# Expert layers of a two-layer Perceiver block: first products, their sums with bias and activations kept four deep, the second product one job later, and function tables called for at the heads of stages

## The reference, cut to what matters

```
def _L0_ffn_ref(x, Wg, alpha, ln_w, ln_b, fc1_w, fc1_b, fc2_w, fc2_b):
    top_vals, top_idx = jax.lax.top_k(logits, TOP_K)
    ...
    for e in range(Wg.shape[1]):
        hdn = _layernorm(xf, ln_w[e], ln_b[e])
        a = jax.nn.gelu(hdn @ fc1_w[e] + fc1_b[e], approximate=True)
        y = a @ fc2_w[e] + fc2_b[e]
        out = out + y * comb[:, e:e + 1]
```

## Time and profile before

| | us |
|---|---|
| median of 3 runs | 1574.12 |
| lowest and highest run | 1567.26, 1579.7 |
| profiled execution, its own time | 1572.63 |
| its span, first to last instruction | 1570.8 |
| busy PE, PE weight loads, DVE, ACT, POOL | 1264.7, 1097.8, 996.1, 841.9, 835.7 |
| mean granted clock of PE | 0.899 of full speed |

### The profile page before, as it was taken

The page is one execution under the profiler, slowest core; times in us unless marked ns, Lnnn a source line. Parts: engine busy times, 40 slices in busy tenths (PEclk is TensorE's granted clock), DMA queues, the critical chain, the costliest instruction groups (busy, mean ns, idle before and its releaser), DMA issues. The chain is left out here.

```text
span 1570.8 us, 48801 instructions
## 1 busy us (share of the span) xinstructions
PE 1264.7 (81%) x15330; PEld 1097.8 (70%) x15331; DVE 996.1 (63%) x3247; ACT 841.9 (54%) x2658; POOL 835.7 (53%) x1700
## 2 busy tenths in 40 slices
PE   3877788989729996799999999999969878449991
PEld 2655777878629886577777777777758767349991
DVE  4655367877346664577777777777759888433334
ACT  1555256565314443577777777777737665224450
POOL 2555024666636564466666666666534566646661
PEclk9999578788559998899999999999979999569996
DMA  7998552121112121312111111111000000122215
GB/s 223 261 263 218 213 165 76 58 63 53 35 49 73 59 62 37 113 62 91 33 50 33 50 34 43 40 37 43 15 15 3 16 24 23 45 61 68 70 58 169
DMA packets 91997, 122.01 MB, mean 78 GB/s; under 512 B 12689, under 2 KB 67218, under 8 KB 91858
## 3 DMA queue, kind: packets, MB, share of 16 engines
q1 hardware_dynamic: 74194, 82.77, 17.8%
q0 software_dynamic: 12288, 34.82, 7.4%
q10 hardware_dynamic: 5376, 2.63, 0.6%
HBM read 89.68 MB, written 30.49 MB: 76 GB/s over the span
## 5 line engine op out<-in xcount | busy, mean ns | idle before, releaser
L1592 ACT ACTIVATE p_prob<-six,p_nm 128x257 f32<-128x257 f32 x512 | 236.4, 475 | 132.1 <-DVE p_nm L1634 122.2
L1634 DVE TENSOR_REDUCE p_nm<-six 128x2 f32<-128x514 f32 x256 | 164.8, 686 | 12.9 <-PE six L1495 12.8
L1842 PE MATMUL bank<-sb_w,m_experts_aT 128*128 x1152 | 156.6, 279 | 7.6 <-ACT m_experts_aT L1871 4.9
L1821 POOL DMA_INDIRECT expert_outputs<-m_experts_y,m_experts_dest x144 | 142.7, 991 | 25.9 <-POOL m_experts_tiny L1820 11.4
L1858 PE MATMUL six<-m_experts_xT,m_experts_w 128*128 128x128 f32 x1152 | 156.0, 279 | 0.0
L1516 PEld LDWEIGHTS six<-sb_const,p_prob 128*128 128x128 f32 x1024 | 109.5, 141 | 65.5 <-issue 59.1
L1516 PE MATMUL six<-sb_const,p_prob 128*128 128x128 f32 x1024 | 137.0, 277 | 19.3 <-issue 17.5
L1842 PEld LDWEIGHTS bank<-sb_w,m_experts_aT 128*128 128x128 f32 x1152 | 141.1, 193 | 13.0 <-issue 12.8
L776 POOL DMA_INDIRECT expert_inputs<-p_r_x,p_r_slot x128 | 126.0, 984 | 41.2 <-issue 34.5
L1375 POOL TENSOR_TENSOR p_score<-p_score,p_mx 128x512 f32<-128x512 f32 x64 | 67.2, 1049 | 147.8 <-DVE p_mx L1320 145.9
L1858 PEld LDWEIGHTS six<-m_experts_xT,m_experts_w 128*128 128x128 f32 x1152 | 143.3, 196 | 0.6 <-issue 0.2
(11 more groups left out here) (287 smaller groups left out, 3498.2 us busy)
## 6 DMA issues: line engine op xcount, KB each, us to landing
ctxN_ring<-ctxN POOLq DMA_DIRECT2D x32, 516.0 KB, 10.6
ctxT_ring<-ctxT SPq DMA_DIRECT2D x32, 514.0 KB, 12.4
p_ctxT<-ctxT SPq DMA_DIRECT2D x32, 514.0 KB, 3.6
m_experts_x<-expert_inputs SPq DMA_DIRECT2D x144, 64.5 KB
bd_scores<-p_rows SPq DMA_DIRECT2D x32, 256.0 KB, 2.8
p_bd<-bd_scores SPq DMA_DIRECT2D x32, 256.0 KB
sb_w<-w SPq DMA_DIRECT2D x32, 256.0 KB
p_y<-expert_outputs SPq DMA_DIRECT2D x32, 128.0 KB, 3.3
```

What stands on the lines that cost most here:

```text
L1592: last = nc.scalar.activation(prob[:, b, g, :], scores_ps[:, g, 0:CTX], ACT.Exp, bias=nm[:, b % 2, g:g + 1], accum_out=total[:, b % 2, g:g ...
L1634: nc.vector.tensor_reduce(nm[:, b % 2, g:g + 2], scores_ps[:, g:g + 2, 0:CTX], AX.X, ALU.max, negate=True).then_inc(s[most], 1)
L1821: nc.gpsimd.indirect_dma_start(m.ys_dram[:, :], bass.IndirectOffsetOnAxis(ap=dest[:, t.par:t.par + 1], axis=0), y[:, t.par, :], None).then ...
L1842: last = nc.tensor.matmul(ps[6 + t.two][:, 0:D], aT[:, t.two, f * P:(f + 1) * P], m.w2[:, DS(held[p] + f * D, D)], start=(f == 0), stop=(f ...
```

## The change

`SECOND` goes from 4 to 5, so S and y of a job come one slot later; POOL's scatter follows (`at(SECOND + 2)`). `h` and `aT` get four buffers instead of two, and F writes banks 2 to 5 in turn instead of 2 and 3; the waits that guard them look four jobs back (`DEEP`). `w` and `xT`, and the banks of T and S, stay two deep. DVE reads 12 values for a group of eight jobs instead of 11, PE 8 as before.

In each `experts` stage and in `cross_many_heads`, ACT gets one more instruction at the head of its queue, a gelu or an Exp of one column of constants into `first_use`, which nothing reads.

```
+            nc.scalar.activation(first_use[:, :], c[:, 0:1], ACT.Exp)
...
-    FIRST, SECOND, STAGES = 1, 4, 6
+    FIRST, SECOND, STAGES, DEEP = 1, 5, 7, 4
...
-        tiny = sb("tiny", [P, 1])
-        w, h, aT = (sb(n, [P, 2, F]) for n in ("w", "h", "aT"))
+        tiny, first_use = sb("tiny", [P, 1]), sb("first_use", [P, 1])
+        w, h, aT = sb("w", [P, 2, F]), sb("h", [P, DEEP, F]), sb("aT", [P, DEEP, F])
+        deep = lambda t: t.par % DEEP
...
-                t = at(6)
+                t = at(SECOND + 2)
...
-                        last = nc.tensor.matmul(ps[6 + t.two][:, 0:D], aT[:, t.two, f * P:(f + 1) * P],
+                        last = nc.tensor.matmul(ps[6 + t.two][:, 0:D], aT[:, deep(t), f * P:(f + 1) * P],
...
-                    if t.past(2):
-                        pe.wait_ge(s["h" if biased else "aT"], t.before(2))
+                    if t.past(DEEP):
+                        pe.wait_ge(s["h" if biased else "aT"], t.before(DEEP))
                     for f in range(FC):
-                        last = nc.tensor.matmul(ps[2 + t.two][:, f * P:(f + 1) * P], w[:, t.two, f * P:(f + 1) * P],
+                        last = nc.tensor.matmul(ps[2 + deep(t)][:, f * P:(f + 1) * P], w[:, t.two, f * P:(f + 1) * P],
...
+            nc.scalar.activation(first_use[:, :], m.const[:, 0:1], gelu)
...
-                    if t.past(2):
-                        act.wait_ge(s["y_ps"], t.before(2))
-                    nc.scalar.activation(aT[:, t.two, :], h[:, t.two, :] if biased else ps[2 + t.two][:, :],
+                    if t.past(DEEP):
+                        act.wait_ge(s["y_ps"], t.before(DEEP))
+                    nc.scalar.activation(aT[:, deep(t), :], h[:, deep(t), :] if biased else ps[2 + deep(t)][:, :],
...
-                    if t.past(2):
-                        dve.wait_ge(s["aT"], t.before(2))
+                    if t.past(DEEP):
+                        dve.wait_ge(s["aT"], t.before(DEEP))
```

More of the change, by code:

```diff
@@ L1442, in cross_many_heads @@
         nm, total = (sb(n, [P, 2, G]) for n in ("nm", "total"))
+        first_use = sb("first_use", [P, 1])
         recip = sb("recip", [P, 2, G])
@@ L1912, in work @@
                     dve.wait_ge(s["h_ps"], t.nth())
-                    if t.past(2):
-                        dve.wait_ge(s["aT"], t.before(2))
+                    if t.past(DEEP):
+                        dve.wait_ge(s["aT"], t.before(DEEP))
                     by_chunk = lambda ap: ap.rearrange("p (f n) -> p f n", f=FC)
-                    nc.vector.tensor_tensor(by_chunk(h[:, t.two, :]), by_chunk(ps[2 + t.two][:, :]),
+                    nc.vector.tensor_tensor(by_chunk(h[:, deep(t), :]), by_chunk(ps[2 + deep(t)][:, :]),
                                             m.bias[:, DS(held[p + SECOND - 2] + D, FC)].unsqueeze(2).broadcast_to(
```

## The result

| | before | after |
|---|---|---|
| median of 6 runs each, us | 1573.45 | 1589.9 |
| lowest and highest | 1567.26, 1579.7 | 1585.79, 1595.79 |
| profiled execution, its span | 1572.63, 1570.8 | 1591.97, 1590.2 |

The ratio is 1.0107, with a 95% interval of 1.0082 to 1.0132. The change makes the kernel slower by 16 to 17 us. I had forecast 1564.7 us and a range up to 1573, and had given slower by over 1% a chance of 0.05.

The account below looks back on a forecast made before the run. PE's weight loads set the pace, but layer 0's experts lag 12.36 us because second products wait for gelu behind DVE's pauses. Gain 8.9 less 1.0 for stage ends is 7.9: 1572.6 to 1564.7 us, range 1558 to 1573.

Parts of the forecast that it names:

- What is late next: Layer 0 experts: once gelu's wait goes, DVE's w delays the first product; 3.5 us of the 12.36 stay.
- the prediction's own sign: Prediction wrong if the first product waits for w in most slots, or layer 0's jobs 3 to 71 stay over 140 us.
- Layer 1: I take 0: Layer 1 experts: no gain, bounds 0 and 0.5 us; a doubled head of PE would cost about 4 us over both layers.
- the pauses of DVE reach nobody in layer 1: Layer 1 experts: there is no h and ACT reads PSUM itself, so DVE's pauses hold up no engine.
- 8.9: Layer 0 experts: PE ends the stage 8.9 us sooner, 12.4 at most and 5.4 at least.
- the prediction's own sums: Layer 0 group heads: w costs 0.1 us now, 0.13 more with 12 values; 0.24 for each of 8 heads, 1.9 us.
- The table loads: Expert stages and cross attention: all three loads of 1.28 us are hidden already, so moving them gives 0.
- the estimate of 8.0 us: Three table switches at the skill page's 2.66 us each, load and drain; not taken, since the trace shows no drain.
- the end of the stages: Both expert stages: three second products in a row delay the last scatter by 0.6 and 0.4 us; cost 1.0, bounds 0 and 1.5.
- C: Rival for layer 0: w takes over and heads and pauses pass to PE in full, 17.8 us for 11.4; 1580.0 us; chance 0.06.
- A: Rival: everything goes, pauses never reach w and table loads were on the path; gain 12.4 plus 3.8, 1556.4 us; chance 0.14.
- B: Rival: nothing to be seen, layer 0's gaps have another cause or later stages give the gain back; 1572 to 1574 us; chance 0.15.

Follow-up runs that it names:

- a1_aligned: Changed kernel with every table entry moved one place (AROUND 9), so reads start at 8 half + 4 again; 1572.74 us, ratio 0.9959.
- d1_pe_read: Changed kernel with PE alone reading 12 values from the aligned place 8 half, DVE still 12 from 8 half + 3; ratio 1.0147.
- e1_control: The kernel before, unchanged, run and profiled once more; 1575.43 us, ratio 1.0014.
- e4_changed_again: The changed kernel, unchanged, run once more beside the kernel before on the same chip; 1591.24 us, ratio 1.0121.
- b3_heads: The kernel before with only the three calls for function tables at the heads of stages added; 1575.73 us, ratio 0.9995.
- e3_order_alone: The kernel before with only the second product one job later and reads held aligned (AROUND 9), two buffers, no table calls; 1567.57 us, ratio 0.9957.
- c1_late_two: a1_aligned with two buffers instead of four, the second product still one job later; 1526.0 us on another chip, ratio 0.9969.
- d2_dve_read: Changed kernel with DVE alone reading 16 values from the aligned place 8 half, PE still 8 from 8 half + 3; ratio 1.0095.
- e2_place_two: The kernel before with AROUND 6, so each group's reads start at 8 half + 2; 1595.46 us, ratio 1.0145.
- b1_shifted: The kernel before with its table one place further (AROUND 9), so reads start at 8 half + 5; 1598.95 us, ratio 1.0128.

## Why the prediction was wrong

**The step that failed** is in the part What is late next: "DVE will read 12 values instead of 11: by 1.47 / 11, 0.13 us more". I took a read's price as proportional to its number of values, and took PE's read, "8 as before" in the account of the change, as free of change. In fact the change moved where both reads start, and that I had before me: `experts_of` has `SECOND` in it twice, in the window's length, which I counted, and in its start, which I didn't. Measured, DVE's read went from 1.336 to 2.851 us and PE's from 0.593 to 1.986. For DVE's eight heads the term was 8 times 0.13, 1 us; for PE there was none. The two reads together cost 12.3 us of layer 0's steady part (a1_aligned). By the prediction's own sign it is wrong: the distance in layer 0 stayed over 140 us.

The second wrong number follows from it: "Layer 1: I take 0", with a gain as the only bound and a doubled head as an aside. Layer 1 lost 8.6 us. A PE at 99% has no cover for anything at its queue's head, so its steps there needed as careful a reading as DVE's. That the pauses of DVE reach nobody in layer 1 is wrong too: DVE's slow read alone costs 7.0 us there (d1_pe_read), through w.

**The ledger** of the two profiled spans, 19.4 us:

| part | after less before, us |
|---|---|
| layer 0, first transpose to last second product's end (154.62, 157.69) | +3.1 |
| layer 1, the same (142.25, 149.99) | +7.7 |
| last scatter behind it, layers 0 and 1 | +1.75, +1.4 |
| start of the cross attention stage | +1.2 |
| gap ahead of the second experts (44.7, 45.8) | +1.1 |
| second self attention (188.7, 192.6) | +3.9 |

These come to about 20.1 us; small differences in other stages take off the rest. The last two rows lie within what the control shows without any change (45.6 and 194.4 us), and the second self attention's is chance by the pair e1_control and e4_changed_again. In the first row two things of opposite sign stand together: the slow reads cost 12.3 us of layer 0's steady part (146.83 less a1_aligned's 134.50), and the rest of the change gains 7.8 there (142.33 less 134.50), both across chips.

**Right, point by point.** That second product, gelu and h stop layer 0, and that one job more of distance takes that away: the waits put down to gelu fall from 4.5 us (8 times) to 1.0 (3 times) in a1_aligned, and with the reads aligned the stage comes to 134.5 us, as forecast. The weight loads of the second product show it better. Their waits in layer 0's steady part, before and in a1_aligned:

```profile
PEld bank L1842 <- issue: 10.3, 21, 1.3
PEld bank L1846 <- issue: 3.0, 6, 0.6
```

Term by term: from the first transpose to the end of the last second product a1_aligned needs 145.01 us, 9.6 less than before, where I had 8.9; 7.8 of them lie in the steady part. But the credit is not all mine: DVE's read, aligned and of 12 values, takes 0.86 us against the 1.34 of 11 before, which gave back 0.48 us at each head that I had not counted. By the prediction's own sums w was late by 0.1 to 0.24 us at each of 8 heads, so 1 to 2 us of the gain is an estimate of what that gave. The kernel before with an aligned read of 12 values was not run, so no run separates it from the order. Layer 1 stays at 130.85 in a1_aligned. The table loads give nothing (b3_heads); the estimate of 8.0 us that I had worked out from the Trainium skill, ScalarE: Activation LUTs, section What ACT_TABLE_LOAD costs, would have been a ratio of 0.995, below the interval's low end of 0.9963. The calls stand where I said, the load at the head of the stage and first work unmoved by it. ACT's timeline in layer 0:

```profile
458.95 1.28 ACT L1869 ACT_TABLE_LOAD   x1 [18.95 <-PEq L1995]
460.25 0.20 ACT L1869 ACTIVATE m_experts_first_use<-sb_const 128x1 f32<-128x1 f32 x1
462.09 0.28 ACT L1884 ACTIVATE m_experts_xT<-six 128x128 f32<-128x128 f32 x1 [1.64 <-PE six L1854]
```

**Mis-sized: the end of the stages.** I had 0.6 and 0.4 us for the last scatter's falling behind. It started 0.85 and 1.11 us after the end of the last second product before, and 2.60 and 2.52 in the changed kernel: 1.75 and 1.41 us. POOL's timeline at the end of layer 1:

```profile
1553.31 0.98 POOL L1825 DMA_INDIRECT expert_outputs<-m_experts_y,m_experts_dest  x1 [0.16 <-issue]
1555.14 0.18 POOL L1824 TENSOR_TENSOR m_experts_tiny<-sb_const 128x1 f32<-128x1 f32 x1 [0.85 <-DVE m_experts_y L1908]
1555.48 0.98 POOL L1825 DMA_INDIRECT expert_outputs<-m_experts_y,m_experts_dest  x1 [0.16 <-POOL m_experts_tiny L1824]
1556.49 0.20 POOL L1824 TENSOR_TENSOR m_experts_tiny<-sb_const 128x1 f32<-128x1 f32 x1
1556.85 0.98 POOL L1825 DMA_INDIRECT expert_outputs<-m_experts_y,m_experts_dest  x1 [0.16 <-issue]
```

The scatters do come 1.37 us apart at the closest, but POOL idled for 0.85 us ahead of the last but one, for y. So DVE was late as well; why, no run shows. In a1_aligned's layer 0, where no read stands in the way, DVE idles for 1.96 us there, with two y made back to back:

```profile
606.83 0.29 DVE L1905 TENSOR_TENSOR m_experts_y<-bank,sb_bias 128x128 f32<-128x128 f32 x1 [0.23 <-PE bank L1846]
609.07 0.49 DVE L1905 TENSOR_TENSOR m_experts_y<-bank,sb_bias 128x128 f32<-128x128 f32 x2 [1.96 <-PE bank L1846]
```

**The rivals.** C gave 1580 us and the right sign. It isn't what happened: its mechanism was DVE's usual pauses passing to w, and with those pauses in place and the reads aligned the stage is quicker, not slower. What it had right is that w is next in line for DVE's lateness, which d1_pe_read shows. A and B fell with the forecast.

**Left open.** Why a1_aligned's layer 0 stays 3.7 us behind its layer 1, and e3_order_alone's 3.1, where c1_late_two on its chip shows 0.5. How much of the gain is the order's and how much the quicker read of 12 values. What makes DVE pause by 1 to 2 us away from the heads. The start of the cross attention stage, where POOL's first use of loaded data comes 2.0 to 4.2 us after the load's start in different kernels, with no relation to the edit that I can see (2.55 before, 2.03 in e3_order_alone, 3.75 in the changed kernel). And whether the limit is a table place divisible by four or an address divisible by 16 bytes: the table's own place in memory was not varied, only the place within it, and of the places that aren't divisible by four only 8 half + 2, 3 and 5 were tried.

## What to carry to other kernels

When a pipeline's depth changes, look for every address that is worked out from it, register reads at loop heads above all. Hold their start at a multiple of four values by padding the table; rather read a few values too many than start off the multiple. And if PE or DVE idles at each loop head behind "issue", look for the register read in the raw trace, since the views of busy time don't show it. Try one change of order without its extras (depth, early calls): here the order, with its read at an aligned place, gave as much as the whole (e3_order_alone).

## What the runs showed of the hardware

The price of a register read from SBUF by a loop's engines, medians of all reads of a trace but the first, 19 for each engine (the first takes 0.1 to 0.25 us longer, 0.776 us for PE before):

| start | PE | DVE |
|---|---|---|
| 8 half + 4, before | 8 in 0.593 us (0.589 to 0.608) | 11 in 1.336 (1.290 to 1.412) |
| 8 half + 4, a1_aligned | 8 in 0.595 | 12 in 0.859 |
| 8 half, d1_pe_read, d2_dve_read | 12 in 0.849 | 16 in 1.164 |
| 8 half + 2, e2_place_two | 8 in 1.976 | 11 in 2.651 |
| 8 half + 3, after | 8 in 1.986 (1.932 to 2.060) | 12 in 2.851 (2.747 to 2.967) |
| 8 half + 5, b1_shifted | 8 in 1.990 | 11 in 2.573 |

Two numbers fit all of it, worked out from these rows: four values from an aligned place cost about 0.29 us together, and a value that isn't in such a four costs 0.23 to 0.25 by itself. 12 are three fours (0.86), 11 are two fours and three single values (2 times 0.29 and 3 times 0.25, 1.33), and an unaligned read of 8, 11 or 12 comes out as that many single ones, though whole aligned fours lie inside it. Twelve values are cheaper than eleven.

The Trainium skill, Runtime: NRT & Kernel Launch, section Instruction fetch mechanics, gives about 200 ns a register, even in bulk, for a TENSOR_LOAD; the page describes it as a load of registers from HBM, and the reads here are from SBUF. For single values the rows come near (0.25 us); in aligned fours they don't (0.07 each), and the difference between the two was this change's whole loss. For reads from SBUF the measurement decides. By the page's figure the 11 values of before would be an estimate of 2.2 us, and its row has 1.34.
